# Gated recurrence: GpSimd multiplies the step sizes into the small matrices, and both first fills become one

## The chip, the cores and the metric

The kernel runs on one core of one Trainium2 chip. The metric is the device time in microseconds (us) of one execution. Five engines run from their own in-order queues and meet at semaphores: TensorE (PE in the profile), VectorE (DVE), ScalarE (ACT), GpSimd (POOL) and SyncE (SP).

## The reference

The whole kernel is a chain of twelve sublayers on 2048 tokens of width 128 (64 sequences of 32 steps). The change touches one, a gated delta-rule recurrence with 16 heads of width 64 and two states per head, S and R:

```python
def step(carry, inp):
    S, R = carry
    q_t, k_t, v_t, a_t, aR_t, b_t, g_t = inp          # a, aR, b (beta), g (gamma) are sigmoids
    kn = k_t / jnp.maximum(jnp.linalg.norm(k_t, axis=-1, keepdims=True), 1e-12)
    pred = jnp.einsum('bhji,bhj->bhi', S, kn)
    r = jnp.clip(v_t - pred, -CLIP, CLIP)
    S = a_t[..., None] * S
    kp = jnp.einsum('bhd,bhde->bhe', kn, S)
    S = S + b_t[..., None, None] * kn[..., None] * (v_t - kp)[..., None, :]
    o = jnp.einsum('bhji,bhj->bhi', S, q_t)
    R = aR_t[..., None] * R
    kpR = jnp.einsum('bhd,bhde->bhe', kn, R)
    R = R + g_t[..., None, None] * kn[..., None] * (r - kpR)[..., None, :]
    o = o + jnp.einsum('bhji,bhj->bhi', R, q_t)
    return ((S, R), o)
```

The step sizes are b_t and g_t, one number per head and token.

## The kernel before

`l1_attn` works on 16 chunks (`NT`) of 128 tokens, that is four sequences of 32 steps. It doesn't run the 32 steps one after another. For each chunk it builds, per head and sequence, small 32x32 matrices of decayed inner products, by TensorE, in five levels (`LEVELS`) of doubling block size. `ms` holds three of them for state S and `mr` two for R, each [32 target steps] per partition (a token), and `ll` the far corners. The part of `ms` and `mr` that multiplies new values is a triangular system, and GpSimd inverts it.

For chunk i the stages are:

- **Projections** (`project_k`, `_q`, `_ar`, `_a`, `_nb`): 128x128 matmuls of a weight by `src`, a copy of the chunk's tokens that ScalarE makes. `project_nb` gives beta and gamma with tokens along the free dimension, and the squared norms of the keys; ScalarE takes sigmoids and a square root (`take_nb`).
- **Keys** (`norms`, `broadcast`, `keys`): VectorE makes 1/norm, beta/norm and gamma/norm in `small` [128, 3, 128]; TensorE spreads them over partitions, eight matmuls with 384 columns into four PSUM banks in turn; VectorE multiplies them with the keys: `rw[:, 1]` is the unit key, `cols[:, 0]` and `cols[:, 1]` are the keys that also carry beta or gamma. ScalarE moves `cols[:, 1]` to `cols[:, 2]` (`move_r`).
- **`begin`**: six VectorE products of the rows `rw` with the gates `a` and `ar` (lines 3413 to 3415, once for each gate).
- **Levels 0 to 4**, once for S and once for R: `fill_s`/`fill_r` on TensorE (line 3174: 64 small matmuls, each of two instruction pairs, so 128 weight loads and 128 matmuls), `keep_s`/`keep_r` on VectorE (predicated copies from PSUM into `ms`, `mr`, `ll`), and `advance` on VectorE, which multiplies decays into `rw` and `cols` in place for the next level (lines 3432, 3434 and 3437 or 3440). Level 0 of S fills 80 columns a block, level 0 of R 64, higher levels 48 and 32.
- **Inverse**: ScalarE copies the triangular parts, negated, to `kc` (`gather`, lines 3008 and 3009), VectorE turns them (`turn`), GpSimd inverts (`merge`, `merge_last`), VectorE turns back (`turn_back`), ScalarE spreads the result to `wideX` (`widen_x`, line 3029).
- **Chain**: `values`, then eight steps y, z, u, p, y2, z2, wr, o of 64 small matmul pairs and more (`apply`, line 3214; `step_o`), with `corner` and `clip` on VectorE between them, then `step_out` and `result`.

Each engine's order is written out by hand in a loop over i in which three chunks are in work: levels 0 to 4 of chunk i, projections and keys of chunk i+1, the inverse of chunk i-1, and the chain of chunk i-2. The VectorE loop starts with `keep_s(i, 0)` and ends with

```python
                if new:
                    norms(i + 1)
                if mid:
                    turn_back(i - 1)
                ...
                if now:
                    keep_s(i, 4)
                if new:
                    keys(i + 1)
                if now:
                    keep_r(i, 4)
                if new:
                    begin(i + 1, a, 0, 2, "rowS")
                    begin(i + 1, ar, 6, 5, "rowR")
```

GpSimd's loop holds only the three merges of a chunk, which wait for `turn`. The next write of `kc` waits until `widen_x` of the chunk before has read it.

## Time and profile before

| | us |
|---|---|
| median of 3 runs | 3036.23 |
| lowest and highest of the 3 | 3035.22, 3039.76 |
| span of the profiled execution | 3029.5 |
| TensorE busy in the span | 2443.0 (81%) |
| VectorE busy | 2046.8 (68%) |
| ScalarE busy | 1381.3 (46%) |
| GpSimd busy | 958.9 (32%) |

The span goes from the first to the last instruction. Of the profiled execution no other time is given, so the median of the runs stands 6.7 us above its span, and that difference is taken as fixed. Busy shares are averages over twelve sublayers; the recurrence is the stretch from about 877 to 2010 us. `norms` (line 3384) runs once a chunk and is used here as the mark of a step.

### The profile page before, as it was taken

How to read it: one execution, taken by the hardware profiler on the slowest of the kernel's cores; microseconds unless marked ns; L12 is line 12 of the kernel's file. 1: busy time of each engine (PE TensorE's matmuls, PEld its weight loads, DVE VectorE, ACT ScalarE, POOL GpSimd, SP SyncE). 2: the span in 40 equal slices, each digit the busy share in tenths (PEclk: the TensorE clock that was granted, in tenths of full speed). 3: DMA queues.
4: the chain of work that ended last, by engine and by line, in shares of the span. 5: the costliest groups of instructions: out<-in, count | busy, mean ns of one | idle time of the engine just before them, and what ended most of it. 6: DMA issues, size and time to landing. Idle time of an engine off the chain costs nothing. (4 is left out here: it accounts for less than half of the span.)

```text
span 3029.5 us, 119908 instructions
## 1 busy us (share of the span) xinstructions
PE 2443.0 (81%) x51995; PEld 1879.4 (62%) x51995; DVE 2046.8 (68%) x4945; ACT 1381.3 (46%) x3266; POOL 958.9 (32%) x1170
## 2 busy tenths in 40 slices
PE   8978477999976787877888787659998997798754
PEld 6755465555555576767767676547876554576633
DVE  3448336777748988989888889257777666664752
ACT  5443233444443445544444443437776554463420
POOL 0000324665640633344333344211111441261004
PEclk9979778999988899999999998879999998897876
DMA  3200431111110000000000000002222003242014
GB/s 100 63 1 29 122 105 53 46 46 46 46 62 3 4 4 4 5 4 4 4 4 4 4 4 4 3 17 60 63 60 67 3 3 106 59 110 68 6 42 120
DMA packets 80349, 118.09 MB, mean 39 GB/s; under 512 B 11360, under 2 KB 66160, under 8 KB 79296
## 3 DMA queue, kind: packets, MB, share of 16 engines
q1 hardware_dynamic: 71312, 100.66, 10.7%
q0 software_dynamic: 8576, 10.53, 1.7%
q8 instruction: 381, 6.24, 0.8%
q14 instruction: 80, 0.66, 0.1%
HBM read 98.51 MB, written 16.51 MB: 38 GB/s over the span
## 5 line engine op out<-in xcount | busy, mean ns | idle before, releaser
L3174 PE MATMUL psum<-l1d_rw,l1d_cols 64*32 64x32 f32 (+2 forms) x20480 | 244.4, 216 | 107.7 <-issue 88.1
L3174 PEld LDWEIGHTS psum<-l1d_rw,l1d_cols 64*32 64x32 f32 x20480 | 211.8, 108 | 151.2 <-issue 126.9
L2469 POOL TENSOR_SCALAR l1xs_p<-l1xs_p,l1xs_col 128x257 f32<-128x257 f32 x256 | 233.8, 932 | 204.7 <-DVE l1xs_col L2425 204.7
L2894 POOL TENSOR_TENSOR l1d_tmp<-l1d_lt,l1d_xi 128x64 f32<-128x64 f32 (+1 forms) x96 | 41.7, 463 | 634.0 <-DVE l1d_xi L3525 632.7
L2390 ACT ACTIVATE l1xs_p<-psum,l1xs_col 128x257 f32<-128x257 f32 x256 | 120.0, 474 | 209.1 <-DVE l1xs_col L2420 203.1
L3432 DVE TENSOR_TENSOR l1d_rw<-l1d_rw,l1d_tots 128x1536 f32<-128x1536 f32 x96 | 151.9, 1582 | 45.7 <-PE psum L3174 45.2
L2432 DVE STREAM_TRANSPOSE l1xs_pt<-l1xs_p 128x288 f32<-128x288 f32 x256 | 122.4, 478 | 79.4 <-POOL l1xs_p L2469 79.4
L3111 PE MATMUL psum<-l1d_src,l1d_wp 128*128 128x128 f32 x1024 | 139.0, 293 | 3.2 <-issue 1.9
L2354 PE MATMUL psum<-l1xs_pt,l1xs_vals 32*128 32x512 f32 x1152 | 136.6, 604 | 0.0
L2342 PE MATMUL psum<-l1xs_keys,l1xs_qx 128*32 128x257 f32 x2048 | 130.9, 389 | 4.3 <-DVE l1xs_qx L2414 2.8
L3111 PEld LDWEIGHTS psum<-l1d_src,l1d_wp 128*128 128x128 f32 x1024 | 128.4, 204 | 7.4 <-issue 4.1
L2634 PE MATMUL psum<-consts,l2x_p 128*86 128x128 f32 x768 | 119.2, 279 | 0.8 <-ACT l2x_pt L2693 0.5
L2719 ACT ACTIVATE l2x_p<-psum,l2x_top 128x257 f32<-128x257 f32 x256 | 118.5, 477 | 0.2 <-DVE l2x_top L2757 0.2
L1986 POOL TENSOR_TENSOR l2a_phi<-l2a_pos,l2a_ex 128x512 f32<-128x512 f32 x64 | 79.9, 1270 | 117.4 <-ACT l2a_ex L1972 117.4
L2693 DVE COPY l2x_pt<-psum 86x384 f32<-86x384 f32 x128 | 70.8, 553 | 47.7 <-PE psum L2634 38.0
L2420 DVE TENSOR_REDUCE l1xs_col<-psum 128x1 f32<-128x257 f32 x256 | 101.1, 409 | 1.8 <-PE psum L2342 1.6
L2580 POOL TENSOR_TENSOR l2x_lane<-l2x_rec,l2x_pick 128x128 f32<-128x128 f32 x64 | 25.5, 399 | 236.1 <-DVE l2x_rec L2764 131.2
L3214 PE MATMUL psum<-l1d_ya,l1d_wideX 64*64 64x64 f32 x2048 | 76.8, 237 | 28.3 <-DVE l1d_ya L3535 26.0
L2323 PEld LDWEIGHTS psum<-XN,l1x_wqk 128*128 128x128 f32 x512 | 66.9, 204 | 47.4 <-issue 32.6
L3434 DVE TENSOR_TENSOR l1d_cols<-l1d_cols,l1d_tots 128x512 f32<-128x512 f32 x96 | 94.6, 986 | 0.0
L2342 PEld LDWEIGHTS psum<-l1xs_keys,l1xs_qx 128*32 128x32 f32 x2048 | 61.2, 110 | 53.4 <-issue 23.4
L2354 PEld LDWEIGHTS psum<-l1xs_pt,l1xs_vals 32*128 32x128 f32 x1152 | 54.5, 184 | 62.7 <-issue 62.5
(558 smaller groups left out, 6845.5 us busy)
## 6 DMA issues: line engine op xcount, KB each, us to landing
l2f_w<-in_l2f_w SPq DMA_DIRECT2D x16, 768.0 KB
l1xs_vals<-in_ctx_strips SPq DMA_DIRECT2D x16, 576.0 KB
l0f_w<-in_l0f_w SPq DMA_DIRECT2D x15, 579.0 KB
l0x_ctxT<-in_ctxT SPq DMA_DIRECT2D x16, 516.0 KB, 3.7
l1xs_keys<-in_ctxT SPq DMA_DIRECT2D x16, 516.0 KB
l2x_ctxK<-in_ctxT SPq DMA_DIRECT2D x64, 129.0 KB, 2.1
l2x_ctxV<-in_ctxT SPq DMA_DIRECT2D x64, 129.0 KB, 2.1
l3f_w<-in_l3f_w SPq DMA_DIRECT2D x15, 193.5 KB
```

Source lines behind the costliest of these rows:

```text
L2342: mm = nc.tensor.matmul(score_ps(t)[32 * c:32 * c + 32, :S2], qx[:, g % 2, n, 32 * c:32 * c + 32], keys[:, g % 2, c, :S2], start=True, sto ...
L2354: mm = nc.tensor.matmul(u_ps[c][:], vals[r, g % 2, j, :], pt[r, g % 2, :, j, :], start=(j == 0), stop=(j == STRIP - 1))
L2390: nc.scalar.activation(p[:, t % 4, :S2], score_ps(t)[:, :S2], ACT.Exp, bias=col[:, 0, t % 4:t % 4 + 1], accum_out=col[:, 1, t % 4:t % 4 + ...
L2420: nc.vector.tensor_reduce(col[:, 0, t % 4:t % 4 + 1], score_ps(t)[:, :S2], AX.X, ALU.max, negate=True).then_inc(s["mx"], 1)
L2432: nc.vector.transpose(pt[:, g % 2, n].rearrange("p j r -> p (j r)"), p[:, t % 4, :]).then_inc(s["pt"], 1)
L2469: nc.gpsimd.tensor_scalar(p[:, t % 4, :S2], p[:, t % 4, :S2], col[:, 2, t % 4:t % 4 + 1], None, ALU.mult).then_inc(s["norm"], 1)
L2634: mm = nc.tensor.transpose(t_ps[j % 2][:KC, c * 128:(c + 1) * 128], p[:, l, j, c * KC:(c + 1) * KC], k.const("ident"))
L2719: nc.scalar.activation(p[:, l % 2, j, :S2], s_ps[j][:, :S2], ACT.Exp, bias=top[:, l % 2, j:j + 1], accum_out=sums[:, l % 2, j:j + 1]).then ...
L3111: mm = nc.tensor.matmul(k.ps[into + j][:, e * 128:(e + 1) * 128], wp[:, n, c:c + 128], src[:], start=True, stop=True)
L3174: mm = nc.tensor.matmul(k.ps[bank0 + pr + e // per * 2][b * T:b * T + T, e % per * w:(e % per + 1) * w], cols[rr, 2 * n, e * 128 + b * T:e ...
L3432: tt(x, x, over.to_broadcast([128, feats.stop - feats.start, 32 * (16 >> lv), m]), ALU.mult)
L3434: ins = tt(c, c, total(n, gate, lv, 1).to_broadcast(wide), ALU.mult)
```

## The change

- `project_nb` computes beta and gamma with tokens along partitions: the tokens are the stationary operand, `wbg` (now 32 columns) moves, and a second matmul adds the bias. `take_nb` takes one sigmoid of 32 columns into `beta`, and a negated copy beside it. `small` holds only the norms, on 64 partitions.
- `broadcast` spreads only 1/norm: eight matmuls with 128 columns into two banks. `keys` makes only `rw[:, 1]`, in two products; ScalarE copies it twice, to `cols[:, 0]` and `cols[:, 2]` (`columns`).
- `fill_0` replaces level 0 of `fill_s` and `fill_r`: 64 small matmuls of 112 columns, from `rw[:, 1]`. It waits for both `rowS` and `rowR`.
- The step sizes are multiplied in at the end, on GpSimd: `gather` (two products into `kc`, in place of ScalarE's two) and `scale` (three products in place, on `ll`, `ms`, `mr`). They stand ahead of the merges in GpSimd's loop.
- `advance` leaves out blocks that no later level reads. At level 3 that is half of the rows and half of the columns.
- The level-0 and level-4 predicated copies go over two banks in one instruction.
- `turn` moves to the head of VectorE's loop; `keep_r(i, 0)` now stands before `advance_s(i, 0)`. `step_out` and `values` move to the head of TensorE's loop, behind `fill_0`, and `values` is one step later.
- `src` and `srcv` go away: matmuls read the tokens in place.

```diff
+            def gather(i):
+                pool.wait_ge(s["mS"], i * LEVELS + LEVELS)
+                pool.wait_ge(s["mR"], i * LEVELS + LEVELS)
+                pool.wait_ge(s["beta"], i + 1)
+                if i > 0:
+                    pool.wait_ge(s["wideX"], i)
+                at = kc[:].rearrange("p (t c) -> p c t", t=T)
+                minus = beta[:, i % 2, 1].unsqueeze(2).to_broadcast([128, 2 * H, T])
+                tt(at[:, :H, :], ms[:, i % 2, :, 0, :], minus[:, :H], ALU.mult)
+                tt(at[:, H:, :], mr[:, i % 2, :, 1, :], minus[:, H:], ALU.mult).then_inc(s["kc"], 1)
+            def scale(i):
+                plus = beta[:, i % 2, 0]
+                x = ll[:, i % 2].rearrange("p n h t -> p (n h) t")
+                tt(x, x, plus.unsqueeze(2).to_broadcast([128, 2 * H, T // 2]), ALU.mult)
+                x = ms[:, i % 2, :, 1:3, :].rearrange("p h f t -> p h (f t)")
+                tt(x, x, plus[:, :H].unsqueeze(2).to_broadcast([128, H, 2 * T]), ALU.mult)
+                x = mr[:, i % 2, :, 0, :]
+                tt(x, x, plus[:, H:].unsqueeze(2).to_broadcast([128, H, T]), ALU.mult).then_inc(s["scaled"], 1)
             for i in range(NT):
+                gather(i)
+                scale(i)
                 pool.wait_ge(s["turn"], 2 * i + 2)
...
             def take_nb(i):
-                for j in range(2):
-                    activation(small[:, 1 + j, :], k.ps[6][:, j * 128:(j + 1) * 128], ACT.Sigmoid, bias=bgcol[:, j:j + 1])
-                activation(small[:, 0, :], k.ps[7][:, :128], ACT.Sqrt).then_inc(s["nb"], 1)
+                activation(beta[:, i % 2, 0], k.ps[6][:, :2 * H], ACT.Sigmoid).then_inc(s["sigm"], 1)
+                activation(small[:], k.ps[7][:64, :128], ACT.Sqrt).then_inc(s["nb"], 1)
+                act.wait_ge(s["sigm"], i + 1)
+                nc.scalar.mul(beta[:, i % 2, 1], beta[:, i % 2, 0], -1.0).then_inc(s["beta"], 1)
...
+            def fill_0(i):
+                if i > 0:
+                    pe.wait_ge(s["mS"], i * LEVELS)
+                    pe.wait_ge(s["mR"], i * LEVELS)
+                pe.wait_ge(s["rowS"], i * LEVELS + 1)
+                pe.wait_ge(s["rowR"], i * LEVELS + 1)
+                fill(rw[:, 1].rearrange("p g t -> p (g t)"), 0, 7, 0, 0, 112, 4).then_inc(s["m0_mm"], 1)
...
             def norms(i):
                 dve.wait_ge(s["nb"], i + 1)
-                n = Steps(dve, s["norm"], i, 2)
-                n(vc.tensor_scalar(small[:, 0, :], small[:, 0, :], 1e-12, None, ALU.max))
-                n(vc.reciprocal(small[:, 0, :], small[:, 0, :]))
-                tt(small[:, 1:3, :], small[:, 1:3, :], small[:, 0:1, :].to_broadcast([128, 2, 128]), ALU.mult
-                   ).then_inc(s["small"], 1)
+                n = Steps(dve, s["norm"], i, 1)
+                n(vc.tensor_scalar(small[:], small[:], 1e-12, None, ALU.max))
+                vc.reciprocal(small[:], small[:]).then_inc(s["small"], 1)
             def keys(i):
...
-                        tt(rw[:, 1, 4 * p:4 * p + 4, :], k.ps[turned[p % 4]][:, :128].rearrange("p (b t) -> p b t", b=TB),
-                           kk[:, p, :].rearrange("p (b t) -> p b t", b=TB), ALU.mult).then_inc(s["kr"], 1)
...
-                        tt(cols[:, :2, j * 128:(j + 1) * 128],
-                           k.ps[turned[j % 4]][:, 128:384].rearrange("p (n t) -> p n t", n=2),
-                           kk[:, j:j + 1, :].to_broadcast([128, 2, 128]), ALU.mult).then_inc(s["kn"], 1)
+                for j in range(2):
+                    tt(rw[:, 1, 16 * j:16 * j + 16, :].rearrange("p (c n b) t -> p c n (b t)", c=2, n=2),
+                       k.psum[:, 6:8, j * 256:(j + 1) * 256].rearrange("p n (c t) -> p c n t", c=2),
+                       kk[:, 4 * j:4 * j + 4, :].rearrange("p (c n) t -> p c n t", c=2), ALU.mult).then_inc(s["kn"], 1)
...
             def advance(i, n, gate, feats, lv, mm, done):
+                if lv == 0:
+                    x, over = x[:, :, :, 1:, 0], over[:, :, 1:, 0].unsqueeze(1).to_broadcast([128, f, 32, some])
+                elif lv == LEVELS - 2:
+                    x, over = x[:, :, :, 1], over[:, :, 1].unsqueeze(1).to_broadcast([128, f, 32, m])
...
+                c = half(cols[:, 2 * n].rearrange("p (g t) -> p g t", t=T), lv, 0)[:, :, :some]
...
             for i in range(NT + 2):
-                if now:
-                    keep_s(i, 0)
-                if 3 <= i != NT:
-                    result(i - 3)
-                if now:
-                    advance_s(i, 0)
                 if mid:
                     turn(i - 1)
                 if now:
+                    keep_s(i, 0)
+                if i >= 3:
+                    result(i - 3)
+                if now:
                     keep_r(i, 0)
+                    advance_s(i, 0)
                     advance_r(i, 0)
```

## Rows read from the trace of the kernel before

**Rows 1.** Eleven steps, the first step: us; busy PE, PEld, DVE, ACT, POOL; clock.

```profile
1138.90:1842.60 703.70, 567.48 (x21746) 495.80 (x21742) 607.23 (x1090) 332.88 (x639) 278.79 (x374) 0.94 0.02 4
911.40:959.40 48.00, 32.22 (x1263) 27.29 (x1261) 41.80 (x77) 16.64 (x48) 0.00 (x0) 0.86 0.02 4
```

**Rows 2.** The line of norms: minimum, median, maximum ns, first and last start.

```profile
L3384 DVE TENSOR_SCALAR l1d_small<-l1d_small x16: 227/228/231, 911.4 to 1842.6; 128x128 f32<-128x128 f32 x16
```

**Rows 3.** Waits in the eleven steps: us in total, times, longest.

```profile
PE psum L3174 <- issue: 57.7, 58, 2.4
DVE l1d_rw L3432 <- PE psum L3174: 36.7, 22, 3.8
DVE l1d_small L3384 <- ACT l1d_small L2999: 32.4, 12, 4.8
DVE l1d_ms L3471 <- PE psum L3174: 13.0, 8, 3.2
```

**Rows 4.** VectorE's timeline of one step: start, us, line.

```profile
1393.04 0.23 DVE L3384 TENSOR_SCALAR l1d_small<-l1d_small 128x128 f32<-128x128 f32 x1 [2.87 <-ACT l1d_small L2999]
...
1402.35 1.22 DVE L3413 TENSOR_TENSOR l1d_rw<-l1d_rw,l1d_a 128x1024 f32<-128x1024 f32 x1
...
1406.42 0.69 DVE L3415 TENSOR_TENSOR l1d_rw<-l1d_rw,l1d_ar 128x512 f32<-128x512 f32 x1
1407.78 1.30 DVE L3471 COPY_PREDICATED l1d_ms<-l1d_imask,psum 128x64 f32<-128x64 int32 x8 [0.67 <-PE psum L3174]
...
1409.11 1.93 DVE L3476 COPY_PREDICATED l1d_ms<-l1d_lmask,psum 128x192 f32<-128x192 int32 x4
...
1416.78 1.32 DVE L3504 COPY_PREDICATED l1d_mr<-l1d_lmask,psum 128x256 f32<-128x256 int32 x2
...
1436.94 1.01 DVE L3544 TENSOR_SCALAR l1d_rd<-l1d_rd 128x512 f32<-128x512 f32 x1
...
1454.94 0.23 DVE L3384 TENSOR_SCALAR l1d_small<-l1d_small 128x128 f32<-128x128 f32 x1 [2.17 <-ACT l1d_small L2999]
```

**Rows 5.** Timelines of VectorE and of GpSimd over the same 5 us.

```profile
1369.66 1.91 DVE L3432 TENSOR_TENSOR l1d_rw<-l1d_rw,l1d_tots 128x1536 f32<-128x1536 f32 x1 [0.31 <-PE psum L3174]
1371.49 1.99 DVE L3434 TENSOR_TENSOR l1d_cols<-l1d_cols,l1d_tots 128x512 f32<-128x512 f32 x1
1373.51 1.59 DVE L3440 TENSOR_TENSOR l1d_tots<-l1d_tots 128x128 f32<-128x128 f32 x1
...
1369.91 4.94 POOL L2923 TENSOR_TENSOR l1d_tmp<-l1d_xi,l1d_wmat 128x512 f32<-128x512 f32 x2
```

**Rows 6.** Single lines over the whole run: minimum, median, maximum ns.

```profile
L3434 DVE TENSOR_TENSOR l1d_cols<-l1d_cols,l1d_tots x96: 678/786/2043, 937.1 to 1900.9; 128x512 f32<-128x512 f32 x96
L2871 POOL TENSOR_TENSOR X<-X,XN x4: 1261/1265/1268, 884.9 to 889.5; 128x512 f32<-128x512 f32 x4
L2921 POOL TENSOR_TENSOR l1d_tmp<-l1d_lt,l1d_xi x32: 1502/1549/2591, 989.7 to 1929.9; 128x512 f32<-128x512 f32 x32
L2925 POOL TENSOR_TENSOR l1d_tmp<-l1d_tmp x64: 718/908/1704, 993.7 to 1937.5; 128x256 f32<-128x256 f32 x64
L3543 DVE TENSOR_TENSOR l1d_rd<-psum,l1d_v x32: 652/679/692, 1055.6 to 1971.1; 128x512 f32<-128x512 f32 x32
L3397 DVE TENSOR_TENSOR l1d_rw<-psum,l1d_cols x128: 276/282/293, 914.1 to 1850.6; 128x128 f32<-128x128 f32 x128
L3402 DVE TENSOR_TENSOR l1d_cols<-psum,l1d_cols x128: 410/415/419, 914.5 to 1851.1; 128x256 f32<-128x256 f32 x128
```

**Rows 7.** ScalarE's timeline at a step's start, and TensorE's at level 0.

```profile
1390.80 0.63 ACT L2998 ACTIVATE l1d_small<-psum,l1d_bgcol 128x128 f32<-128x128 f32 x2 [7.48 <-PE psum L3152]
...
1395.91 4.08 ACT L3029 ACTIVATE l1d_wideX<-l1d_kc,l1d_part 128x1024 f32<-128x1024 f32 x2 [0.93 <-DVE l1d_kc L3529]
...
1405.99 1.64 PE L3174 MATMUL psum<-l1d_rw,l1d_cols 64*32 64x80 f32 x128
...
1412.54 1.50 PE L3174 MATMUL psum<-l1d_rw,l1d_cols 64*32 64x64 f32 x128
```

**Rows 8.** DMA queues in the eleven steps: packets, MB, share.

```profile
q8 instruction: 171, 2.80, 1.6%
```

More of the change, by code:

```diff
@@ L3311, in _ @@
             project_a(0)
-            broadcast(0, 0)
-            broadcast(0, 4)
-            fill_s(0, 0)
+            broadcast(0)
+            fill_0(0)
             for i in range(NT + 2):
                 now, old, mid, new = i < NT, 0 <= i - 2 < NT, 0 <= i - 1 < NT, i + 1 < NT
+                if 3 <= i <= NT:
+                    step_out(i - 3)
+                if old and i <= NT:
+                    values(i - 2)
                 if new:
                     project_q(i + 1)
-                if now:
-                    fill_r(i, 0)
                 if old and i != NT + 1:
```

317 lines of the change are left out of this document (134 added, 183 removed).

## The prediction

> **What bounds the kernel now.** I read the page first, then busy time by stretch, then the waits inside the recurrence, then the timelines of one step. The page names no engine as the bound. Inside the recurrence it is plainer: from 1138.9 on, eleven steps from one run of `norms` to the next (a mark) take 703.70 us, 63.97 each, in which VectorE is busy 55.2, TensorE 51.6, ScalarE 30.3 and GpSimd 25.3 [rows 1]. (607.23, 567.48, 332.88 and 278.79, each by 11.) There are 16 marks, 911.4 to 1842.6 [rows 2], one for each chunk. VectorE's 8.8 us of idle time a step are mostly waits for fills, 36.7/11 = 3.3 us at line 3432 and 13.0/11 = 1.2 at level 0, and for the square root, 32.4/11 = 2.9 [rows 3]. So VectorE's chain, with three or four hand-overs to TensorE and ScalarE, sets a step.
>
> Two more things count. TensorE stands still without a visible reason for 57.7 us in its fills [rows 3], 5.2 a step. In the same stretch 171 instruction packets of 16 KB arrive, one each 4.1 us [rows 8]. I read these stops as TensorE outrunning its instruction supply; that is an inference. Then GpSimd and VectorE get in each other's way: while two GpSimd products of 512 elements take 4.94 us (1.50 is the least for such a one), VectorE's 512-element product takes 1.99 instead of 0.68 and a 128-element one 1.59 [rows 5, 6]. The ends fit strict turns: GpSimd's first product waits out VectorE's at 1369.66, VectorE's at 1371.49 waits for that one, GpSimd's second waits for VectorE's, and the one at 1373.51 for GpSimd's second. VectorE ops that read PSUM go on (line 3543 takes 652 to 692 ns throughout [rows 6]). By the Trainium skill ("SBUF — State Buffer", Who interferes with whom) this is an exclusive lock: a VectorE instruction with two SBUF inputs and a GpSimd one that reads SBUF shut each other out for a whole instruction. The rows agree, and the rule speaks against the change, since it puts five more GpSimd instructions beside six VectorE products that all read two SBUF tensors. The sum below goes by the rows alone.
>
> **The sum for one step, along VectorE.** I follow the step that starts at 1393.04. `begin` starts 9.3 after it and ends 14.1 after it, `keep_s(0)` starts at 14.7, the last clip ends at 44.9, the next mark is at 61.9 [rows 4]. The tail from clip to mark is 17.0.
>
> *Head.* `norms` 1.2 (its third product goes, 0.4), `turn_back` 1.2, `keep_s(4)` 1.1, `keep_r(4)` 0.7 stay. `keys` now is eight pairs of 0.28 and 0.41 that start 0.53 apart, 4.25, plus about 1 us of waiting for banks in turn; it becomes two PSUM products of 512 elements, 0.66 each by line 3543 [rows 6], 1.3. `broadcast` is ready, since it now runs at once behind `small`. `begin` starts at 5.5 instead of 9.3.
>
> *The lock in `begin`.* `gather` may start when `keep_r(4)` is done (5.5) and when `widen_x` has read `kc`. That read starts about 2.9 after a mark and takes 4.08 [rows 7]; with `turn_back` 0.4 earlier it ends at 6.6. Then GpSimd has two products of 512 elements, one of 512, one of 1024 and one of 512 in a row. No row shows them. A plain 512-element product takes 1.265, one with strided operands 1.50 [rows 6], so 2.5 to 3.0 ns an element; I take 2.5, since the larger part is contiguous. VectorE is then in the second of its six products; before the sixth ends, four of GpSimd's have had their turns, 2560 elements, 6.3 us (7.7 at the upper end; 0 if they don't exclude each other, which the rows make unlikely). `begin` ends at 5.5 + 4.8 + 6.3 = 16.6, 2.5 later than now. The Trainium skill ("GPSIMD Engine Reference", Elementwise — side-by-side cycle accounting) gives 2.6 cycles an element at 1.2 GHz; by this estimate, 2.2 ns, the four would take 5.5, not 6.3.
>
> *Fill.* `fill_0` waits for both gates. Fills of 64 and 80 columns take 1.50 and 1.64 [rows 7]; two more such steps of 16 give 1.9 for 112 (3.8 at half clock). `turn`, 1.5, lies beside it. `keep_s(0)` starts at 18.6, against 14.7.
>
> *Level 0 to keep_s(1).* The predicated copies keep their elements in half as many instructions: 1.3 and 1.7 for S (1.30 and 1.93 now), 1.3 and 1.1 for R (1.32 for its second half now) [rows 4]; with `result`, 0.2, they lead to 24.1. Then three `advance` stand in a row, nine products with two SBUF inputs and 6624 elements. The six of `begin` have 4096 in 4.8 us [rows 4], 1.16 ns each, so these take 7.5 to 7.7 alone. The merges have started behind `turn` at 18.4; by 24.1 they are at the 512-element ones. Turn by turn VectorE lets pass about one of 1.5, two of 0.72, two of 0.4, two of 0.3 and one more of 1.5: 6.3 us (today the merges meet VectorE partly beside PSUM copies and cost it about 4.3 a step). This ends at 37.9. `keep_s(1)` 1.7 and `corner` 1.3: 40.9.
>
> *To the clip.* `advance_r(1)`, 1728 elements, 2.0 and 0.6 of lock; `keep_r(1)` 1.2; `advance_s(2)`, 2048 elements, 2.4; clip 2.1 (its clamp, 1.01 beside the merges [rows 4], takes half when they are done): 49.2. TensorE has u, `fill_s(2)` and p to do behind `corner`; with its supply stops I add 0.6. Clip ends at 49.8, against 44.9.
>
> *Tail.* `advance_s(3)` loses 768 row and 256 column elements, 1.07 us, but `fill_r(3)` and its stop then decide, so I count half. The beta and gamma matmuls lose 0.2 and the sigmoids 0.4 of their 0.63 [rows 7]. 17.0 becomes 15.5. The step is 49.8 + 15.5 = 65.3, 1.3 more than the mean of 63.97.
>
> **Other edits.** Ahead of VectorE's chain they cost nothing: ScalarE has 33 us free a step, which covers the second `columns` copy (1.07); if that were gone it would cost 1.07. `step_out`, `values` and `project_q` behind `fill_0`, 6 us on TensorE, lie beside the level-0 copies; `fill_s(1)` behind them needs `advance_s(0)`, which is later still. TensorE loses 256 of some 3950 instructions a step (21746 + 21742 by 11 [rows 1]) and the wide broadcasts; that is room on an engine that isn't the bound. SyncE only loads one more small mask before the loop.
>
> **Whole kernel.** Thirteen steps of the full kind: +17. The first step, 48.0 with GpSimd idle [rows 1], has the savings and no lock: -6. The second has the lock and no chain: +1. The end: in the drain `scale` stands before the merges that everything waits for, 2048 elements, 5.1 us, of which `turn` hides 1.6, so 3.5; the later clip of the last steps and a `gather` that I take to be somewhat slower than ScalarE's add as much: +7 together. Sum +19 on the profiled 3029.5, and the same on the median: 3036 + 19 = 3055.
>
> **Rivals.**
> - *The lock doesn't bite in `begin`* (faster). If GpSimd's products came after `begin`, or ran beside it, the step is 65.3 - 6.3 = 59.0, and then TensorE's supply sets a floor: about 14.4 packets instead of 15.5 at 4.1 less some slack, 59 or 60. Thirteen steps at -4 and +2 at the ends: 2986. For it: 6 us of VectorE's own work really go (3.0 keys, 2.5 advance, 0.6 small ones). Against it stand the turns in [rows 5]. It decides from the point where `begin` is stretched by less than 5 us. Part of it, a lock of half the size, gives 3015.
> - *No change.* Savings and lock cancel, 5 us of lock in `begin`: 3030 to 3042.
> - *GpSimd is slower than thought and TensorE cools down* (much slower). The write into `kc` has a stride of 128 bytes; at 3.0 ns an element or more, +1.4, and TensorE, idle from about 8 to 16.6 before `fill_0`, comes back at 1.2 GHz instead of 2.4 (the mean granted clock is 0.94 now, 0.86 in the emptier first step [rows 1]), +1.9 in `fill_0`. With 1.3 more of slower merges: +4.6 a step over mine, 3055 + 60, about 3110.
> - *TensorE's supply sets the second half* (slower): 1600 instructions lie from u to `project_nb`, 6.25 packets; at 3.6 us or so they need 22 us where I leave 18 to 20. +2 a step: 3081. It is the upper half of my own case.
>
> **Chances.** My case with the supply rival, 3043 to 3092: 0.53. Lock that doesn't bite or only in part, 2980 to 3029: 0.26. No change: 0.09. Much slower: 0.12. The likeliest has its own range of 3043 to 3092; for 8 in 10 I take 2998 to 3100. Under 0.2% (6 us) a change can't be told from none by this kernel's runs. Slower 0.65, within 0.09, faster 0.26.
>
> **What would show it.** In the trace after: lines of `begin` at well over 1.22 and 0.69 us, turn by turn with GpSimd; level-0 copies about 18 us behind a mark; `keys` 1.3 us; lines 3432 of level 3 halved; GpSimd busy 33 us a step or more; a step of about 65. The prediction is wrong if `begin` still takes 4.8, or if the idle time of VectorE falls well below 7 us a step.

## The result, and the profile after

The changed kernel takes 3131.97 us (median of 4 runs, 3130.63 to 3142.07), the kernel before on the same chip 3035.72: 1.032 times as long, 95% interval 1.030 to 1.034, or 96 us. I had forecast 3055, with a range of 2998 to 3100. Slower was right, the size was not: 77 us are missing.

The profiled execution took 3130.63 us, 1.8 more than its span of 3128.8. So the 6.7 us that I had taken as a fixed difference is none: the kernel before was profiled in an execution that was faster than each of its timed runs. In the profiled execution a step takes 71.5 us instead of 64.0. Busy time by stretch, first step and eleven steps (columns as in [rows 1]):

```profile
912.00:960.00 48.00, 27.45 (x996) 25.32 (x994) 34.34 (x53) 15.47 (x44) 0.00 (x0) 0.72 0.01 3
1160.20:1947.10 786.90, 577.44 (x20335) 525.86 (x20330) 600.70 (x803) 319.04 (x607) 348.20 (x429) 0.83 0.01 3
```

VectorE is busy 54.6 us a step (55.2 before), TensorE 52.5 (51.6) although it issues 256 instructions fewer, and GpSimd 31.7 (25.3). TensorE's mean granted clock is 0.83, against 0.94 in [rows 1]: more of the stretch lies at 1.2 GHz, less at 2.4. The waits in these eleven steps (as [rows 3]):

```profile
DVE l1d_rw L3426 <- PE psum L3174: 88.0, 41, 5.0
PE psum L3174 <- DVE l1d_rw L3396: 69.9, 11, 6.9
PE psum L3174 <- issue: 46.8, 45, 2.4
DVE l1d_small L3373 <- ACT l1d_small L3018: 36.5, 11, 4.8
DVE l1d_ms L3459 <- PE psum L3174: 28.4, 11, 3.5
PE psum L3174 <- DVE l1d_tots L3431: 26.0, 11, 3.5
```

VectorE now waits 8.0 us a step for fills at its advance line instead of 3.3, and TensorE waits 6.4 us a step for `begin` ahead of `fill_0` and 2.4 for `advance` ahead of `fill_s(1)`. Neither of these two rows has a counterpart before. The instruction queue brings 160 packets instead of the 171 of [rows 8], in a longer time:

```profile
q8 instruction: 160, 2.62, 1.4%
```

VectorE's timeline of the step from 1375.10 to 1446.96 (as [rows 4]):

```profile
1375.10 0.22 DVE L3373 TENSOR_SCALAR l1d_small<-l1d_small 64x128 f32<-64x128 f32 x1 [3.56 <-ACT l1d_small L3018]
...
1379.57 1.29 DVE L3383 TENSOR_TENSOR l1d_rw<-psum,l1d_cols 128x512 f32<-128x512 f32 x2 [1.20 <-PE psum L3162]
1382.76 0.44 DVE L3504 COPY_PREDICATED l1d_mr<-l1d_lmask,psum 128x256 f32<-128x256 int32 x1 [1.90 <-PE psum L3174]
...
1383.43 1.22 DVE L3394 TENSOR_TENSOR l1d_rw<-l1d_rw,l1d_a 128x1024 f32<-128x1024 f32 x1
1384.56 1.54 DVE L3395 TENSOR_TENSOR l1d_rw<-l1d_rw,l1d_a 128x512 f32<-128x512 f32 x1
1386.03 1.53 DVE L3396 TENSOR_TENSOR l1d_rw<-l1d_rw,l1d_a 128x512 f32<-128x512 f32 x1
1387.48 2.07 DVE L3394 TENSOR_TENSOR l1d_rw<-l1d_rw,l1d_ar 128x1024 f32<-128x1024 f32 x1
1389.48 2.38 DVE L3395 TENSOR_TENSOR l1d_rw<-l1d_rw,l1d_ar 128x512 f32<-128x512 f32 x1
1391.78 1.53 DVE L3396 TENSOR_TENSOR l1d_rw<-l1d_rw,l1d_ar 128x512 f32<-128x512 f32 x1
...
1397.63 1.31 DVE L3459 COPY_PREDICATED l1d_ms<-l1d_imask,psum 128x128 f32<-128x128 int32 x4 [2.94 <-PE psum L3174]
...
1424.60 1.76 DVE L3426 TENSOR_TENSOR l1d_rw<-l1d_rw,l1d_tots 128x1536 f32<-128x1536 f32 x1 [2.72 <-PE psum L3174]
...
1438.24 0.96 DVE L3426 TENSOR_TENSOR l1d_rw<-l1d_rw,l1d_tots 128x768 f32<-128x768 f32 x1 [4.07 <-PE psum L3174]
```

GpSimd in the same step:

```profile
1383.67 1.93 POOL L2943 TENSOR_TENSOR l1d_kc<-l1d_ms,l1d_beta 128x512 f32<-128x512 f32 x1 [38.09 <-DVE l1d_ll L3505]
1385.52 1.50 POOL L2944 TENSOR_TENSOR l1d_kc<-l1d_mr,l1d_beta 128x512 f32<-128x512 f32 x1
1386.97 1.50 POOL L2950 TENSOR_TENSOR l1d_ll<-l1d_ll,l1d_beta 128x512 f32<-128x512 f32 x1
1388.43 2.88 POOL L2952 TENSOR_TENSOR l1d_ms<-l1d_ms,l1d_beta 128x1024 f32<-128x1024 f32 x1
1391.27 1.49 POOL L2954 TENSOR_TENSOR l1d_mr<-l1d_mr,l1d_beta 128x512 f32<-128x512 f32 x1
```

`keys` is down to 1.3 us and the five products take turns with `begin` as forecast: the 512-element products of `begin` take 1.53 us instead of 0.69, and the one that meets GpSimd's 1024 elements 2.38. `begin` takes 9.9 us instead of 4.8. Now TensorE in the same step, and its granted clock (the last column but two) in three stretches of it:

```profile
1393.46 3.20 PE L3174 MATMUL psum<-l1d_rw 64*32 64x112 f32 x119 [6.88 <-DVE l1d_rw L3396]
1396.90 0.60 PE L3174 MATMUL psum<-l1d_rw 64*32 64x112 f32 x9 [0.24 <-issue]
...
1407.72 1.73 PE L3174 MATMUL psum<-l1d_rw,l1d_cols 64*32 64x48 f32 x128 [2.23 <-DVE l1d_tots L3431]
...
1427.06 3.05 PE L3113 MATMUL psum<-XN,l1d_wp 128*128 128x128 f32 x16
```

```profile
1375.10:1381.10 6.00, 4.70 (x293) 4.25 (x288) 4.53 (x8) 5.61 (x7) 0.00 (x0) 1.00 0.02 5
1381.10:1399.10 18.00, 9.67 (x273) 8.72 (x274) 13.32 (x15) 5.74 (x9) 12.88 (x19) 0.53 0.01 2
...
1407.10:1420.00 12.90, 10.97 (x384) 10.33 (x386) 12.87 (x13) 3.21 (x7) 11.00 (x12) 0.74 0.02 4
```

For 17 of the 18 us in the second row TensorE is granted half its clock: it is half idle there, then comes `fill_0` as the first thing that VectorE waits for, 4.0 us from first to last. In the other steps the stretch at half clock around `fill_0` is 7 to 21 us long, and the whole of `fill_0` or nearly so lies in it each time (3.7 us on the mean). What is late by then stays late: 16 projection matmuls take 3.05 us at 1427.06 (2.05 at the full clock), and the last fills keep VectorE waiting 2.72, 1.07 and 4.07 us.

### The profile page after: what moved, and what is told of

Same layout as the page of the kernel before. It is cut to its first block and busy times, and to the rows that moved or that the text cites. A ratio compares the mean times of both kernels' runs of the same rounds, so it can differ in the third digit from the quotient of the medians.

```text
span 3128.8 us, 115484 instructions
## 1 busy us (share of the span) xinstructions
PE 2451.9 (78%) x49947; PEld 1915.8 (61%) x49947; DVE 2029.4 (65%) x4529; ACT 1356.4 (43%) x3218; POOL 1058.1 (34%) x1250
## 5 line engine op out<-in xcount | busy, mean ns | idle before, releaser
L3174 PE MATMUL psum<-l1d_rw,l1d_cols 64*32 64x48 f32 x16384 | 190.8, 215 | 120.8 <-issue 68.4
L3174 PEld LDWEIGHTS psum<-l1d_rw,l1d_cols 64*32 64x32 f32 x16384 | 167.3, 111 | 140.9 <-issue 128.8
L2943 POOL TENSOR_TENSOR l1d_kc<-l1d_ms,l1d_beta 128x512 f32<-128x512 f32 x16 | 28.6, 1787 | 607.5 <-DVE l1d_ll L3505 511.6
L3426 DVE TENSOR_TENSOR l1d_rw<-l1d_rw,l1d_tots 128x1536 f32<-128x1536 f32 (+1 forms) x96 | 126.7, 1320 | 116.3 <-PE psum L3174 116.0
L3174 PE MATMUL psum<-l1d_rw 64*32 64x112 f32 x2048 | 54.8, 384 | 114.5 <-DVE l1d_rw L3396 111.2
L3113 PE MATMUL psum<-XN,l1d_wp 128*128 128x128 f32 x1024 | 142.4, 297 | 1.1 <-ACT XN L226 1.0
L3113 PEld LDWEIGHTS psum<-XN,l1d_wp 128*128 128x128 f32 x1024 | 132.0, 208 | 12.8 <-issue 9.2
L3174 PEld LDWEIGHTS psum<-l1d_rw 64*32 64x32 f32 x2048 | 46.8, 152 | 119.0 <-issue 119.0
L3211 PE MATMUL psum<-l1d_ya,l1d_wideM 64*64 64x64 f32 x2048 | 85.1, 246 | 22.4 <-issue 17.0
L3211 PEld LDWEIGHTS psum<-l1d_ya,l1d_wideX 64*64 64x64 f32 x2048 | 76.7, 159 | 41.0 <-DVE l1d_ya L3524 37.5
L2693 DVE COPY l2x_pt<-psum 86x384 f32<-86x384 f32 x128 | 70.8, 553 | 46.5 <-PE psum L2634 36.9
```

Source lines behind the costliest of these rows:

```text
L3113: mm = nc.tensor.matmul(k.ps[into + j][:, e * 128:(e + 1) * 128], wp[:, n, c:c + 128], tokens(i), start=True, stop=True)
L3174: mm = nc.tensor.matmul(k.ps[bank0 + pr + e // per * 2][b * T:b * T + T, e % per * w:(e % per + 1) * w], columns[rr, at:at + T], moving[rr ...
L3211: mm = nc.tensor.matmul(k.ps[bank(name) + h // 8][rr, (h % 8) * 64:(h % 8 + 1) * 64], lhs(h)[rr], rhs[rr, h * 64:(h + 1) * 64], start=base ...
L3426: tt(x, x, over, ALU.mult)
```

## The experiments

Each kernel is timed against the kernel before on the same chip. Chips differ by up to 0.6% (the kernel before: 3035 to 3053 us), so ratios are compared, with their 95% intervals; 0.01 is 30 us. I use two measures of my own from the records. **Milestones** are means over the last twelve steps, in us after a mark. **Stops and waits** are TensorE's gaps of over 0.1 us between two records, per step over eleven: a stop lies inside one group of matmuls, a wait ahead of a group.

```
                   ratio   begin from-to  keep_s(0)  corner end  clip end  step | stops waits
before             1       10.2  15.0     16.2       35.0        46.9      63.7 |  7.9   4.3
after              1.0324   7.4  17.3     21.3       42.7        52.5      71.2 |  6.5  12.4
e1_noprod          1.0213   7.3  12.0     19.9       40.5        50.6      68.9 |  7.5   9.6
e2_vector          1.0181   7.2  11.9     17.9       39.6        49.9      68.1 |  7.7   9.2
e5_old_pool        1.0191  10.3  20.2     20.1       38.9        50.9      67.9 |  8.2   6.6
e6_old_cuts        0.9978  10.4  15.2     16.6       35.2        47.7      64.8 |  8.4   4.0
e9_split_free      1.0132   7.5  12.3     14.9       37.9        51.1      68.0 |  9.5   5.9
e10_split_noprod   0.9932   7.6  12.3     15.0       33.9        47.5      64.4 | 11.2   2.4
e17_join_clean     1.0024   7.5  12.2     16.2       37.4        47.3      66.8 |  8.2   7.0
```

A profile is one execution; e17_join_clean's (3071.93 us) is its slowest of twelve, so its step reads some 0.9 us long. Ratio and step can also differ because the loop isn't all of the kernel. The profiled execution of e10_split_noprod has a span of 3022.7, 6.8 us less than that of the kernel before, but its eleven steps take 6.9 us more; what it gains lies in its first four steps (5.6 us) and behind its last mark (9.2).

### The lock, the waits and the order in the changed kernel

**e1_noprod**: without the five products; ScalarE negates into `kc` as before.

```diff
-                gather(i)
-                scale(i)
                 pool.wait_ge(s["turn"], 2 * i + 2)
```

> The changed kernel without its five GpSimd products: ScalarE negates the triangular parts into kc as the kernel before did, and nothing is multiplied by beta or gamma, so the output lacks the step sizes. Theory L (the products and VectorE's two-input products take turns in begin): begin falls from 9.9 to 4.8 us, the step from about 71.5 to 64 to 66.5, the whole to 3020 to 3060. Rival Q (the merged first fill and the new queue orders are what costs; the lock hides beside them): begin falls too, but fill_0, its wait and the second half stay, and the whole stays above 3095.

3100.26 us, ratio 1.021 (1.018 to 1.025). `begin` is back at 4.8 us, and only a third of the loss goes. That spoke for the rival, wrongly, as e17_join_clean shows below: the profile has a wait of the experiment's own making,

```profile
1379.54 1.25 DVE L3498 STREAM_TRANSPOSE l1d_lt<-l1d_kc 128x1024 f32<-128x1024 f32 x1 [5.47 <-ACT l1d_kc L3004]
```

since ScalarE's gather stands in its queue behind its copies for `columns`.

**e2_vector**: the five products on VectorE.

```diff
                 if mid:
+                    gather(i - 1)
                     turn(i - 1)
+                    scale(i - 1)
```

> The same five products, issued by VectorE instead of GpSimd: gather before turn, scale behind it. 3072 elements at 1.16 ns are 3.6 us of VectorE's time a step, partly beside fill_0. L: begin 4.8 instead of 9.9, the step 1.5 to 4 us shorter, the whole 3075 to 3110. Q: no gain, since VectorE only gets more work: 3130 or more.

3091.53 us, ratio 1.018 (1.015 to 1.022), in the expected range: 4.6 us a step more of work on VectorE is cheaper than the same products beside `begin`.

**e3_warm**: five matmuls of 512 columns, whose results are overwritten, ahead of `fill_0`'s wait for the gates.

```diff
+                    for _ in range(5):
+                        nc.tensor.matmul(k.ps[0][:], k.const("ident"), wv[:, :512], start=True, stop=True)
                 pe.wait_ge(s["rowS"], i * LEVELS + 1)
```

> Five matmuls of 512 columns into a bank that fill_0 then overwrites, on TensorE while it waits for begin (idle 6.9 us in the step looked at). They change no data. Theory C (TensorE's granted clock falls in that wait, and fill_0 and the matmuls behind it run at 1.2 GHz): the granted clock rises from 0.83 to 0.9 or more, fill_0 takes 1.9 instead of 3.4 us, the whole falls by 20 to 45 us to 3087 to 3112. If the clock costs nothing on the path: 3128 to 3140.

3116.54 us, ratio 1.025 (1.022 to 1.029). The clock of the eleven steps rises from 0.83 to 0.88, and 22 us come back (1.0324 to 1.0253), fewer than the theory wanted: `fill_0` takes 2.7 us on the mean instead of 3.7, not 1.9.

**e4_order**: two groups of matmuls ahead of `fill_0` on TensorE.

```diff
+                if new and i >= 2:
+                    step_out(i - 2)
+                if new and i >= 1:
+                    values(i - 1)
                 if new:
                     fill_0(i + 1)
```

> step_out and values go back ahead of fill_0, into TensorE's wait for begin (2.5 and 1.9 us). L: fill_s(1) waits for advance_s(0) anyway (2.2 us in the step looked at), so nothing is won but what a warmer TensorE gives: 3115 to 3133. Q: the order behind fill_0 was on the path, 4 us a step: 3075 or less.

3115.78 us, ratio 1.026 (1.022 to 1.029): 20 us come back, in theory L's range, and mostly for its reason, the clock. `fill_0` lies at the full clock in all eleven steps and takes 1.94 us instead of 3.67, and `keep_s(0)` starts 1.3 us earlier, where the whole step gains 1.6. That less work queued behind the fill gave something too isn't shown.

**e12_vector_warm**: e2_vector with two such matmuls ahead of `fill_0` and three ahead of `fill_s(1)`.

```diff
+                if lv == 1 and i > 0:
+                    for _ in range(3):
+                        nc.tensor.matmul(k.ps[0][:], k.const("ident"), wv[:, :512], start=True, stop=True)
                 pe.wait_ge(s["rowS"], i * LEVELS + lv + 1)
```

> e2_vector with matmuls of 512 columns whose results are overwritten where TensorE would stand idle: two ahead of the wait for the gates in fill_0, three ahead of the wait in fill_s(1) (about 1.07 us each at 2.4 GHz). Nothing else is changed. Theory C (a part of what e2_vector has left over the kernel before is the clock that falls where TensorE idles): granted clock in the recurrence from 0.88 to 0.93 or more, 1 to 3 us a step less, 3045 to 3080 us. Rival: the clock rises but the step stays, since the fills' own waits set it: 3085 to 3100 us.

3093.01 us, ratio 1.017 (1.014 to 1.020), not distinct from e2_vector's. The clock rose only from 0.88 to 0.90, and the rival's range held. A higher clock by itself doesn't pay where the wait is short.

### One part at a time in the kernel before

**e5_old_pool**: five products of 512, 512, 512, 1024 and 512 elements on a scratch tensor, at the place of the change's.

```diff
             for i in range(NT):
+                pool.wait_ge(s["mS"], i * LEVELS + LEVELS)
+                pool.wait_ge(s["mR"], i * LEVELS + LEVELS)
+                for n in (512, 512, 512, 1024, 512):
+                    dstep(tt(dum[:, :n], dum[:, :n], dum[:, :n], ALU.mult))
                 pool.wait_ge(s["turn"], 2 * i + 2)
```

> The kernel before, with five more GpSimd products (512, 512, 512, 1024, 512 elements, contiguous, on a scratch of their own) placed where the change puts its own: free to start when the last fills are kept, ahead of turn's merges. Their results are not used; each waits for the one before it. Nothing else is changed. Theory L (turn-taking stretches begin, and nothing behind it takes it up): begin takes about 9.5 to 10 us instead of 4.8, a step 3 to 5 us more, 3075 to 3100 us. Rival H (the old order hides it, since its first fill needs only the first gate and the copies behind it wait anyway): under 1.5 us a step, below 3055 us.

3103.93 us, ratio 1.019 (1.017 to 1.021), 58 us: within theory L's 39 to 64 us over the 3036 for which it was written. VectorE's and GpSimd's timelines show the same turns, to 0.01 us, on data that have nothing to do with `begin`'s:

```profile
1373.95 1.54 DVE L3427 TENSOR_TENSOR l1d_rw<-l1d_rw,l1d_a 128x512 f32<-128x512 f32 x1
1375.40 1.52 DVE L3428 TENSOR_TENSOR l1d_rw<-l1d_rw,l1d_a 128x512 f32<-128x512 f32 x1
1376.85 2.06 DVE L3426 TENSOR_TENSOR l1d_rw<-l1d_rw,l1d_ar 128x1024 f32<-128x1024 f32 x1
1378.83 2.38 DVE L3427 TENSOR_TENSOR l1d_rw<-l1d_rw,l1d_ar 128x512 f32<-128x512 f32 x1
...
1373.04 9.06 POOL L2944 TENSOR_TENSOR l1d_dum<-l1d_dum 128x512 f32<-128x512 f32 x5 [24.30 <-DVE l1d_ll L3529]
```

**e6_old_cuts**: `advance` with the change's cuts alone.

```diff
-                ins = tt(c, c, total(n, gate, lv, 1).to_broadcast(wide), ALU.mult)
+                ins = tt(c[:, :, :some], c[:, :, :some], total(n, gate, lv, 1)[:, :, :some].to_broadcast([128, 32, some, m]), ALU.mult)
```

> The kernel before with one part of the change alone: advance leaves the blocks that nothing reads unscaled. Theory V (VectorE's chain sets a step, with the products at 1.1 to 1.2 ns an element): some 2.2 us of products less in a step, of which 0.7 to 1.8 us shorten it, 3012 to 3027 us. Rival T (TensorE with its instruction supply sets the step): within 6 us of the kernel before.

3039.92 us against 3048.57, ratio 0.998 (0.996 to 1.000), 7 us: far nearer to the rival, which allowed 6, than to theory V. VectorE is busy 53.2 us a step instead of 55.2 (585.66 by 11), and waits longer instead. In [rows 3] its wait for the fills was 36.7 us, here it is

```profile
DVE l1d_rw L3440 <- PE psum L3174: 56.4, 30, 4.6
```

**e11_old_join**: the first level of the change alone: one fill of 112 columns behind both gates, `turn` first, `keep_r(0)` ahead of three `advance`. The R part of this fill uses the keys that carry beta in place of those with gamma; the gamma keys are left out of it here and in e16_join_late_turn.

```diff
                 if lv == 0:
-                    fill(0, 0, 5, lv, 0, 80, 4).then_inc(s["mS_mm"], 1)
+                    pe.wait_ge(s["rowR"], i * LEVELS + 1)
+                    fill(0, 0, 7, lv, 0, 112, 4).then_inc(s["mS_mm"], 1)
```

> The kernel before with the first level of the change alone: one fill of 112 columns that waits for both gates and stays in banks 0 to 3, the two-bank copies, turn ahead of keep_s(0), keep_r(0) ahead of three advance in a row, fill_s(1) behind keep_r(0); the stationary of the joined fill is the first of the two scaled key tensors for both parts, so the second part's fill uses beta in place of gamma. Scaled keys, broadcasts, ScalarE's negation and the order of step_out and values stay. Theory A (alone it costs nothing, since TensorE comes to the first fill only when begin is over, at 16.4 us after a mark): within 1 us a step, 3030 to 3060 us on a chip where the kernel before takes 3036 to 3049. Rival J (the joined fill costs time by itself, since fill_s(1) now waits for keep_r(0) and TensorE idles there with its clock falling): 2 us a step or more, 3065 us or more.

3142.30 us, ratio 1.033 (1.029 to 1.036): rival J, and as much as the whole change. In the step looked at, `begin` ends 17.3 us after the mark, but the fill lasts from 17.4 to 21.6 with a supply stop of 2.0 in it, and `turn` starts only at 21.7: it waits for ScalarE's gather, as in every step of this run, 4.4 us a step. Three `advance` take 12.3 us and TensorE waits 4.7 us ahead of `fill_s(1)`.

```profile
DVE l1d_lt L3527 <- ACT l1d_kc L3011: 48.6, 11, 5.3
```

**e16_join_late_turn**: the same with VectorE's old order.

```diff
-                    turn(i - 1)
                     keep_s(i, 0)
                     result(i - 3)
-                    keep_r(i, 0)
                     advance_s(i, 0)
+                    turn(i - 1)
+                    keep_r(i, 0)
                     advance_r(i, 0)
```

> e11_old_join with VectorE's old order: keep_s(0), result, advance_s(0), turn, keep_r(0), advance_r(0), so that the merges start 3 us of products later. fill_s(1) still waits for keep_r(0). In e11_old_join three advance behind turn took 12.3 us, in the kernel before 2.96 and 5.86 about it. Theory A (merges against products are half of it): the step is 2 to 4 us shorter than in e11_old_join, 3085 to 3115 us. Rival J (TensorE's wait ahead of fill_s(1) and the clock behind it are all of it, and keep_r(0) ends as late): 3125 us or more.

3102.37 us, ratio 1.018 (1.017 to 1.020): inside theory A's range, 44 us less than e11_old_join by the ratios. But the old order undoes two things at once: products no longer meet the merges where copies did, and VectorE no longer waits for ScalarE's gather (its waits have no such row). By the records `keep_s(0)` starts 2.9 us earlier (18.1 instead of 21.0 after a mark), and from there to the end of `corner` 18.9 us pass instead of 20.9. So order and wait together are nearly half of that loss, and theory A's reason has at most a part of it; the run doesn't tell them apart.

### The first level as before, in the changed kernel

**e7_split**: e2_vector with two first fills, of 80 and 64 columns, and VectorE's old order.

```diff
-                pe.wait_ge(s["rowR"], i * LEVELS + 1)
-                fill(rw[:, 1].rearrange("p g t -> p (g t)"), 0, 7, 0, 0, 112, 4).then_inc(s["m0_mm"], 1)
+                fill(rw[:, 1].rearrange("p g t -> p (g t)"), 0, 5, 0, 0, 80, 4).then_inc(s["m0_mm"], 1)
+            def fill_1(i):
+                fill(cols[:, 2], 3, 7, 0, 2, 64, 8).then_inc(s["m1_mm"], 1)
```

> e2_vector (the five products on VectorE) with the first level as it was before: a fill of 80 columns that waits for the first gate alone, then, behind project_q, one of 64 columns for the second; on VectorE keep_s(0), result, advance_s(0), then the products and turn, keep_r(0), advance_r(0). The two-bank copies, the unscaled keys, the cuts and the shorter beta path stay. Theory M (the joined fill costs what e2_vector has left over the kernel before: TensorE is idle until both gates are done, then fills slowly, and the copies wait for all of it): keep_s(0) starts 2.5 to 4 us earlier after a mark than the 17.9 of e2_vector, a step of 64 to 66 instead of 68.1 us, 3040 to 3066 us. Rival S (what is left is TensorE in the second half of a step, behind the first copies): 3080 us or more.

3104.99 us, ratio 1.019 (1.017 to 1.020): rival S's range. `keep_s(0)` does start 3.5 us earlier (14.4), but I had left `fill_s(1)` waiting for `keep_r(0)`, and TensorE stood idle 5.0 us a step there.

**e8_split_order**: e7_split with e4_order's diff.

> e7_split with step_out and values of the step ahead of its first fill on TensorE, as in e4_order. Theory M: the same or up to 10 us less than e7_split, since TensorE is idle there; rival S: 10 us or more below e7_split, since this takes 6 us of TensorE's work out of the stretch behind the fill.

3156.29 us, ratio 1.036 (1.033 to 1.039): both missed. What gave 20 us in the changed kernel costs 51 here. The first fill no longer waits, so work put ahead of it delays it: `keep_s(0)` starts at 18.2 instead of 14.4.

**e9_split_free**: e7_split without that wait of `fill_s(1)`.

```diff
-                if lv == 1:
-                    pe.wait_ge(s["mR"], i * LEVELS + 1)
```

> e7_split without one wait that I had left in it: fill_s(1) waited for keep_r(0), which the joined fill needs (both its parts lie in banks 0 to 3) and the split one doesn't. In e7_split that left TensorE idle for 4.98 us a step ahead of the level-1 fills. Theory T (TensorE, with its supply stops and the clock that falls where it idles, is as critical as VectorE, so each wait of TensorE is paid): the idle time goes to under 1 us, z and project_k run at the full clock again, and a step falls from 68.9 to 64 to 66 us: 3040 to 3070 us. Rival V (VectorE sets a step; it carries the products here, about 4.6 us, and saves 3.0 in keys and 2 in advance): under 1 us a step less than e7_split, 3090 us or more.

3085.25 us, ratio 1.013 (1.010 to 1.017): between the two theories. The idle time ahead of the fills goes to 0.25 us, as theory T had it, but the step falls by 0.7 us only (68.9 to 68.3 over the eleven steps).

**e10_split_noprod**: the same without any of the products (the diffs of e1_noprod, e7_split and e9_split_free).

> The same first level (split fill, no wait for keep_r(0), VectorE's old order) with none of the five products: ScalarE negates as before, and nothing is multiplied by beta or gamma (that part of the computation is left out). What is left of the change are its savings. Theory T: with the lock and the joined fill gone, a step is 60.5 to 63.5 us, faster than the 64.0 of the kernel before: 2990 to 3032 us. Rival O (something else in the change costs time: narrower broadcasts that let the clock fall, step_out and values behind the fill, take_v late): 3040 us or more.

3024.52 us against 3039.95, ratio 0.993 (0.990 to 0.996), within theory T's range of times. These are all the savings of the change with nothing against them: 21 us (12 to 29 by the interval). But theory T wanted a step of 60.5 to 63.5 us, and the profile shows 64.6, no less than the 64.0 before: the full steps show no gain. Busy time and waits in its eleven steps:

```profile
1134.30:1844.90 710.60, 559.68 (x21742) 504.30 (x21738) 539.49 (x803) 334.86 (x628) 261.41 (x374) 0.93 0.02 4
```

```profile
PE psum L3159 <- issue: 84.4, 75, 2.4
DVE l1d_rw L3417 <- PE psum L3159: 69.9, 39, 5.4
```

VectorE has 6.2 us a step less to do than in [rows 1] (49.0 against 55.2). TensorE stands 7.7 us a step in supply stops inside its fills instead of 5.2, and VectorE waits 6.4 instead of 3.3.

**e17_join_clean**: e1_noprod with ScalarE's gather ahead of its copies of `o`.

```diff
-                if mid:
-                    gather(i - 1)
...
+                if i < NT:
+                    gather(i)
                 if old:
                     take(i - 2, "o_mm", rd, "B", "o")
```

> e1_noprod with ScalarE's gather ahead of its copies of o, so that turn no longer waits for it: the whole change without the five products (nothing is multiplied by beta or gamma; that is left out), with nothing else in the way. Against e10_split_noprod (ratio 0.993) it shows the joined first level with its order on VectorE, against the changed kernel (1.032) the lock. Theory J (the joined level costs most of it: fill_0 and all nine products of three advance beside the merges lie in one chain, TensorE idles ahead of fill_s(1)): ratio 1.010 to 1.020, 3070 to 3095 us, with fill_0 ending at 16 to 17 us after a mark and fill_s(1) at 31 or later. Rival L (the lock costs most of it, e1_noprod's artifact hid that): below 1.007.

3059.33 us against 3053.05, ratio 1.002 (1.001 to 1.004): rival L. `keep_s(0)` starts at 16.2 instead of 19.9, and this one wait was worth 57 us of e1_noprod's 65. Its busy times:

```profile
1150.50:1888.30 737.80, 568.84 (x20334) 515.37 (x20330) 543.95 (x804) 341.77 (x629) 250.22 (x374) 0.88 0.02 4
```

### What sets a step

Three kernels change `fill_r(2)` of the kernel before, behind which TensorE waits about 3 us for the clip.

```diff
# e14_more                                   # e15_longer
+   fill(1, 5, 7, lv, 2, 32, 8)              +   nc.tensor.matmul(k.ps[2][:], ident, wv[:, :512])
    fill(1, 5, 7, lv, 2, 32, 8)                  fill(1, 5, 7, lv, 2, 32, 8)
# e13_fewer: two matmuls of 256 columns in place of the fill
```

> The kernel before with fill_r(2), 64 matmuls that are 256 instructions in the trace, 1.29 us, replaced by two matmuls of 256 columns of about the same length, 248 instructions fewer in a step (that fill's results are left out). TensorE's busy time stays. Theory F (the instruction supply sets the step): one packet in 15.5 less, 2 to 4 us a step less, 2985 to 3012 us. Rival W (TensorE's work and VectorE's waits set it): within 0.7 us a step, 3030 to 3050 us.

> The kernel before with fill_r(2) issued twice, 256 instructions and 1.29 us more, where TensorE then waits 3.1 us for the clip. Theory F: one packet more, 2 to 4 us a step, 3065 to 3090 us. Rival W: the wait for the clip takes it up, within 0.7 us a step, 3030 to 3055 us.

> The kernel before with one matmul of 512 columns more at the same place, 1.07 us and a few instructions. Control for e14_more. Both theories: within 0.7 us a step, 3030 to 3055 us; if TensorE's busy time were what counts, +1 us a step, 3050 or more, as in e14_more.

e14_more: 3104.12 us, ratio 1.019 (1.017 to 1.022), 58 us or 4.5 a step. e15_longer: 0.999 (0.997 to 1.000). e13_fewer: 1.001 (0.999 to 1.003). So 1.0 us more of matmul there costs nothing, but 256 more instructions cost a whole packet's time, and more than theory F's 2 to 4 us a step. The queue and the supply stops of e14_more's eleven steps:

```profile
q8 instruction: 182, 2.98, 1.7%
```

```profile
PE psum L3174 <- issue: 83.4, 70, 2.5
DVE l1d_rw L3434 <- PE psum L3174: 84.6, 31, 5.9
```

One packet more a step than in [rows 8], and 2.3 us a step more in stops (57.7 in [rows 3]). That the stops are waits for instructions was my inference; the records bear it out. In the kernel before 72 of the 82 stops of over 0.3 us in the eleven steps end between 1.2 and 1.6 us after a packet of this queue has landed (62 of 63 in the changed kernel, 86 of 95 here), where a tenth would by chance. The other direction failed the theory: 248 instructions fewer give nothing. e13_fewer's timeline of TensorE shows where one step's gain goes:

```profile
1385.97 2.05 PE L3111 MATMUL psum<-l1d_src,l1d_wp 128*128 128x128 f32 x16
1387.86 1.03 PE L3204 MATMUL psum<-l1d_wv,consts 128*128 128x256 f32 x4
1391.85 3.68 PE L3218 MATMUL psum<-l1d_rd,l1d_wideX 64*64 64x64 f32 x64 [2.96 <-DVE l1d_rd L3548]
1395.45 3.13 PE L3111 MATMUL psum<-l1d_src,l1d_wp 128*128 128x128 f32 x16
```

Ahead of the wait a projection takes 2.05 us; behind it the next group takes 3.68 (2.08 at the full clock) and the same projection 3.13.

**e18_cuts_early_fill**: e6_old_cuts with one fill earlier.

```diff
+                if now:
+                    fill_s(i, 3)
                 if new:
                     project_a(i + 1)
-                if now:
-                    fill_s(i, 3)
```

> e6_old_cuts with fill_s(3) ahead of project_a on TensorE, since VectorE's cut advance_s(2) and keep_s(2) are done when TensorE comes out of its wait for the clip, and VectorE waits 1.7 us for that fill. Theory T (TensorE's queue sets the tail whatever its order, so VectorE's wait only moves): the same as e6_old_cuts, ratio 0.995 to 1.001. Rival V (VectorE's wait ahead of advance_s(3) is on the path): 1 us a step or more, ratio below 0.993.

3063.92 us against 3053.05, ratio 1.004 (1.002 to 1.005): slower than either theory said. No complete kernel here beats the one before by more than e6_old_cuts, 0.2%.

## Why the prediction was right in sign and wrong in size

**The lock was right.** Turn by turn with GpSimd, `begin` got 5.1 us longer; I had 6.3. VectorE loses 0.84 us to a product of 512 elements and 1.69 to one of 1024, 1.65 ns an element and not the 2.5 that I had from another GpSimd product. In the drain, where no VectorE product of two SBUF tensors lies beside them, the change's own products take this long:

```profile
2022.01 1.06 POOL L2950 TENSOR_TENSOR l1d_ll<-l1d_ll,l1d_beta 128x512 f32<-128x512 f32 x1
2023.03 1.90 POOL L2952 TENSOR_TENSOR l1d_ms<-l1d_ms,l1d_beta 128x1024 f32<-128x1024 f32 x1
```

From the first to the second 512 elements more cost 0.84 us, the same 1.65 ns an element; the 0.2 us that each product takes besides cost VectorE nothing. That 5.1 came near 6.3 is in part luck: the price was lower, but five products had their turns in `begin` and not four. By the Trainium skill ("SBUF — State Buffer", Who interferes with whom) the two shut each other out for whole instructions; the trace agrees in the turns, but part of each GpSimd product lies beside VectorE's.

**The step that failed: "So VectorE's chain, with three or four hand-overs to TensorE and ScalarE, sets a step."** I took off each saving on VectorE at its full length (3.8 us before `begin`, 2 to 3 in `advance`, 1.5 in the tail); the 6 us a step that I counted would be 78 us in thirteen steps. All of them together, with lock and joined fill undone, returned 21 us in the whole kernel and none that shows in the full steps (e10_split_noprod), and the cuts alone 7 (e6_old_cuts). TensorE was as near to the limit as VectorE: in a step of 64.0 it waited 4.3 us for others and the rest was work (51.8) and stops (7.9). I had the supply floor only as a rival's footnote, at 59 or 60; in e10_split_noprod TensorE waits 2.4 us a step for others, and its work and stops fill the other 62.

**Term by term**, forecast and measured (after, means of twelve steps): `begin` starts at 5.5, measured 7.4, since `keys` waited for the broadcast and `keep_r(4)` for a fill (1.20 and 1.90 us in the step shown); I had kept no wait there. `begin` lasts 11.1, measured 9.9. From its end to `keep_s(0)` 2.0, measured 3.9: `fill_0` ran at half clock behind 6.4 us of idleness. From there to `corner`'s end 22.3, measured 21.4: the level-0 copies and the meeting of merges and products were right. To the clip 8.9, measured 9.8. Tail 15.5, measured 18.7: I had let the savings shorten it, but TensorE comes late and slow into it. The differences are the 5.9 us from 65.3 to 71.2, and thirteen steps of it the 77 us. The half clock I had priced in the rival "much slower", but as one fill's 1.9 us, not as 24 us of each step (the mean clock of 0.83; 8 us before) and a late second half.

**The sum had a second fault.** I built it on the step that starts at 1393.04, which takes 61.9, and then held the 65.3 against the mean of 63.97. Against its own step the forecast was 3.4 us more and not 1.3; thirteen times 2.1 are 27 of the 77 us. Taken as changes, the means of twelve steps before and after say where the rest lies: the start of `begin` was forecast at -3.8 and moved by -2.8, `begin` +6.3 and +5.1, the gap to `keep_s(0)` +1.4 and +2.7, from there to the clip +1.0 and +0.5, and the tail -1.5 and +1.9. So the tail is the term that was furthest off, 3.4 us a step or 44 us, and it is the one from which I had taken the small savings of VectorE, ScalarE and TensorE one by one, without TensorE's late start.

**The ends came out by luck.** For the first step I had -6, since it has the savings and no lock; it took 4 us more (52.1 instead of 48.1). It takes 46.5 in e10_split_noprod and 52.6 in e17_join_clean, so what it lost is the joined first level. The second step took 4.7 more where I had 1, but from the last mark to the last result there was 0.1 more where I had 7, and what follows the recurrence was 5 us shorter. These misses nearly cancel.

**Where the 96 us are**, by ratios: the savings -0.7% (21 us, e10_split_noprod), the joined first level with its order on VectorE +0.9% (28 us, 15 to 41 by the two intervals; e17_join_clean over that), the five products on GpSimd +3.0% (91 us, by the two intervals 80 to 102; the change over e17_join_clean). The same products cost 58 us in the kernel before (e5_old_pool). That TensorE's lower clock behind its longer wait has a part in the rest is borne out by e4_order and e3_warm, which both raise it and brought back 20 and 22 us. I haven't run the two together, so how much of the rest it is stays open. The joined level alone cost 1.8 to 3.3% in the kernel before, and 0.9% in the changed one. Part of the 3.3% is VectorE's wait for ScalarE's gather, 4.4 us a step in e11_old_join and absent in e16_join_late_turn and e17_join_clean. Why 1.8% without it stand against 0.9% isn't settled.

My theory after the result, that the lock was most of it, seemed refuted by e1_noprod; I then took the joined level for the cause, and e11_old_join seemed to confirm it. Both runs had `turn` ahead of a late gather on ScalarE. Only e17_join_clean, without that, tells lock and joined level apart.

## What to carry to other kernels

Before a saving on the busiest engine is counted, add up the other engine's work and its stops in a step. Here TensorE had 4 us of slack in 64, and neither 2 us less on VectorE (e6_old_cuts) nor 248 instructions fewer on TensorE (e13_fewer) was worth more than 7 us in all, while 5.1 us of delay in `begin` cost 4.5 a step (e5_old_pool). An experiment that removes a part can bring a wait of its own; look at what ended each idle time before its number is believed. GpSimd's work may cost less beside VectorE's reads of PSUM than beside its products; no run here moved it there.
